# A five-engine kernel whose loop over passes is written out in full

## Chip, cores and metric

The kernel runs on one core of a Trainium2 chip. The metric is the time of one execution on the device, in microseconds. Five engines work side by side: TensorE (PE in the profile, PEld for its weight loads), VectorE (DVE), ScalarE (ACT), GpSimd (POOL) and SyncE (SP), which here issues all DMAs. Each has its own instruction stream, and they hand work to each other through semaphores.

## What is computed

Two transformer layers over 32 sequences of 256 rows with 128 features, each sequence on its own. Every sub-layer is followed by a residual sum and a layer norm:

```python
x = L0_attn_x                                   # (32, 256, 128)
x = _layernorm(x + _L0_attn_ref(x, ...))        # 16 heads of 8, softmax with a distance bias
x = _layernorm(x + _L0_ffn_ref(x, ...))         # 8 experts, top 2, and a shared one; silu(x W1) * (x W3) W2
x = _layernorm(x + _L1_attn_ref(x, ...))        # each row attends to rows at fixed distances; a sigmoid gate
x = _layernorm(x + _L1_ffn_ref(x, ...))         # 8 experts, top 2, one matrix each
return x
```

## The kernel before

One sequence's work is cut into stages, and the stages are laid over each other like a pipeline. `LAG` says how many passes after its start a sequence reaches a stage: `A1` (q, k, v and the scores for the row maximum) and `M` in pass e, `A2` and `A3` (first attention) in e + 1, `B` (experts of the first layer) in e + 2, `B2` in e + 3, `C1` and `C2` (second attention) in e + 3 and e + 4, `D` and `D2` (experts of the second layer) in e + 5 and e + 6. So one pass works on up to seven sequences, and 32 sequences take 38 passes. A pass runs `one(t, par, key)` on every engine: `t` is the pass, `par` its parity (some buffers are double), and `stages(t)` gives the sequence of each stage or None.

Within a pass each engine follows a fixed list of steps, `ORDER`. TensorE begins with `A1.qk` (L423, L424), `A1.v`, `B2.z` (L542) and `D2.y`; VectorE begins with `B2.res` (L956), then the steps of `A1` (L900 to L915), `D2.res` (L950) and `N.root` (L817 to L834), which computes the inverse roots of all four layer norms of the pass. From `n_r` and `n_b` that it gives, ACT normalises (L754), and TensorE transposes the result (L441) for the next stage.

Nothing synchronises the passes but these steps. Each engine counts its finished steps of a stage in a semaphore (`Steps`), and a waiting step waits for `count(e, step)`, which is `e` times the number of steps in a pass, plus the step's place. A finished DMA adds 16 (`dma_count`).

The passes stand in three parts. Passes 0 to 6 (`LOOP_FROM` is 7) are written out. Passes 7 to 30 are a loop on each engine, `eng.Fori`, of 12 turns with two passes each, since parity must be a constant. Passes 31 to 37 (`LOOP_TO` is 31) are written out again. In the loop `t` is an expression of the loop's register:

```python
with eng.Fori(0, (LOOP_TO - LOOP_FROM) // 2) as r:
    for u in range(2):
        one(r * 2 + (LOOP_FROM + u), (LOOP_FROM + u) % 2, LOOP_FROM + u)
```

so each wait's value, and the addresses of three DMAs on SP (`bass.ds(e * T, T)` and the like), are computed in registers while the kernel runs. `take` keeps for each PSUM bank who used it last, and in what pass; where the loop begins and ends its record is set to the loop's terms.

Of the kernel before, what the change touches and what calls it, by code (L numbers as in the profile page):

```python
# [6 lines left out]
B, T, D = 32, 256, 128  # L7
H, HD = 16, 8
E = 8
TT = T // 128  # L10
# [26 lines left out]

NORMS = ("A3n", "B2", "C2n", "D2")
LAST = max(LAG.values())
LOOP_FROM = LAST + 1  # L40
LOOP_TO = LOOP_FROM + (B - 1 - LOOP_FROM) // 2 * 2
Z_FIRST = 6
PV_ORDER = (0, 1, 4, 5, 2, 3, 6, 7)

# [51 lines left out]
def dma_count(e, per_run=1):  # L96

    return 0 if isinstance(e, int) and e < 0 else (e + 1) * (16 * per_run)


def network(nc, A, out):
# [4 lines left out]
    with ctx:  # L106
        def sb(name, shape, dt=F):
            return ctx.enter_context(nc.sbuf_tensor(name, shape, dt))
# [4 lines left out]
        def sem(name):  # L113
            return ctx.enter_context(nc.semaphore(name))
# [22 lines left out]
        xT = sb("xT", [128, T])  # L137
        x0, x2b = sb("x0", [128, TT, D]), sb("x2b", [128, TT, D])
# [13 lines left out]
        xout = sb("xout", [128, TT, D])  # L152
# [91 lines left out]
        ld_xT, ld_x = sem("ld_xT"), sem("ld_x")  # L244
        st_part, ld_stack, ld_m = [sem(f"st_part{n}") for n in range(3)], sem("ld_stack"), sem("ld_m")
        st_cB, ld_cB, st_cD, ld_cD = sem("st_cB"), sem("ld_cB"), sem("st_cD"), sem("ld_cD")
        st_w, ld_w, st_out = sem("st_w"), sem("ld_w"), sem("st_out")
# [11 lines left out]
        x_rows = A["x"].rearrange("b (t p) c -> p (b t) c", p=128)  # L259
        out_rows = out.rearrange("b (t p) c -> p (b t) c", p=128)  # L260
# [13 lines left out]
        def stages(t):  # L274

            r = {}
            for s, lag in LAG.items():
                e = t - lag
                r[s] = None if isinstance(e, int) and not 0 <= e < B + (LAG["D"] - lag if s == "G" else 0) else e
            return r  # L280
# [2 lines left out]

            return slice(0 if r["B"] is not None else 1, 2 if r["D"] is not None else 1)

        def passes(eng, one):


            for t in range(LOOP_FROM):
                one(t, t % 2, t)  # L290
            with eng.Fori(0, (LOOP_TO - LOOP_FROM) // 2) as r:
                for u in range(2):
                    one(r * 2 + (LOOP_FROM + u), (LOOP_FROM + u) % 2, LOOP_FROM + u)
            for t in range(LOOP_TO, B + LAST):
                one(t, t % 2, t)

        block = ctx.enter_context(nc.Block())
# [3 lines left out]
        def _(sp):  # L301
# [15 lines left out]
            def one(t, par, key):  # L317
                r = stages(t)
                for what, n in ORDER["sp"]:
# [2 lines left out]
                            sp.dma_start(dst[:], A[name]).then_inc(ld_expert, 16)  # L322
                    if what == "X.xT" and (e := r["X"]) is not None:
                        sp.wait_ge(peA1.sem, peA1.count(e - 1, "v"))
                        sp.dma_start(xT[:], A["xT"][:, bass.ds(e * T, T)]).then_inc(ld_xT, 16)
                    if what == "A3.x":
                        if (e := r["A3"]) is not None:
                            sp.wait_ge(dveA3.sem, dveA3.count(e - 1, "res"))
                            sp.dma_start(x0[:], x_rows[:, bass.ds(e * TT, TT), :]).then_inc(ld_x, 16)
                    if what == "A1.part" and (e := r["A1"]) is not None:  # L330

                        if n == 0:
# [51 lines left out]
                        sp.dma_start(stack[par][ROW_M:ROW_M + 1, 0], mT[:]).then_inc(ld_m, 16)  # L384
                    if what == "D2.out" and (e := r["D2"]) is not None:
                        sp.wait_ge(actND.sem, actND.count(e, "nm", 1))
                        sp.dma_start(out_rows[:, bass.ds(e * TT, TT), :], xout[:]).then_inc(st_out, 16)

            passes(sp, one)
            sp.wait_ge(st_out, dma_count(B - 1))  # L390


        @block.tensor
        def _(pe):
# [5 lines left out]
            last = {b: None for b in (0, 1, 2, 6, 7)}  # L400
# [6 lines left out]
                last[bank_no] = (*now, t)  # L407

            def one(t, par, key):
                if key == LOOP_FROM and not isinstance(t, int):  # L410
                    for b in last:
                        last[b] = (*last[b][:4], t - 1)
                if isinstance(t, int) and t == LOOP_TO:
                    for b in last:
                        last[b] = (*last[b][:4], LOOP_TO - 1)
                r = stages(t)
                odd = 1 - par
                for what, n in ORDER["pe"]:
# [205 lines left out]
                    if what == "M.mT" and (e := r["M"]) is not None:  # L624
# [5 lines left out]
                            i = nc.tensor.transpose(o[0:H, tt * 128:tt * 128 + 128], mneg[:, tt, :], identb[:])  # L630
                        i.then_inc(peM.done("mT"), 1)

            passes(pe, one)


        @block.scalar
        def _(act):
# [17 lines left out]
            def one(t, par, key):  # L655
# [3 lines left out]
                for what, n in ORDER["act"]:  # L659
# [103 lines left out]
                    if what == "M.mT" and (e := r["M"]) is not None:  # L763
                        act.wait_ge(peM.sem, peM.count(e, "mT"))
                        act.wait_ge(ld_m, dma_count(e - 1))
                        nc.scalar.copy(mT[:], b7[:].bitcast(BF)[0:H, 0:T]).then_inc(actM.done("mT"), 1)

            passes(act, one)


        @block.vector
        def _(dve):
# [273 lines left out]
                        dve.wait_ge(peM.sem, peM.count(e - 1, "mT"))  # L1046
                        v.tensor_scalar(mneg[:], mx[:], -1.0, None, ALU.mult).then_inc(dveM.done("neg"), 1)

            passes(dve, one)


        @block.gpsimd
        def _(pool):
# [50 lines left out]
                        tt_(h9[:, n, :].rearrange("p (t n) -> p t n", t=TT), ub[n % 2][:].rearrange("p (t n) -> p t n", t=TT),  # L1104
                            gB["cb"][:, :, expert(n), :], ALU.mult).then_inc(poolB.done("h", n - 1), 1)

            passes(pool, one)


def distance_tables():  # L1110
# [114 lines left out]
```

## Time and profile before

| | |
|---|---|
| Time of three runs | 1998.36, 2018.55 and 2006.53 us; median 2006.53 us |
| The profiled execution | 2014.43 us, of which 2012.6 us is the span of the program's own instructions |
| TensorE | busy 1601.7 us (80% of the span), mean granted clock 0.905 |
| VectorE | busy 1334.9 us (66%) |
| ACT | busy 922.6 us (46%) |
| POOL | busy 917.0 us (46%) |
| DMA | 214.15 MB, 106 GB/s; two of the queues, q8 and q14, carry instructions |

The time is that of one execution; the profile is another view of one such execution, on the only core used. In its rows a time in square brackets is how long the engine had been idle before, followed by what ended it; "issue" stands there where the profile shows nothing that was waited for. The granted clock (PEclk) is TensorE's share of its full 2.4 GHz; it takes two levels, 1.00 and 0.50, and in a stretch it is their mean.

### The profile page before, as it was taken

The page shows a single profiled execution, that of the slowest core. Times are in us where ns is not written, and L with a number is a line of the kernel's source. Part 1 is how long each engine was busy: PE and PEld are TensorE (multiplying, and loading weights), DVE is VectorE, ACT ScalarE, POOL GpSimd, SP SyncE. Part 2 cuts the span into 40 slices and gives each one's busy share as a digit, 9 for nine tenths or more (in the row PEclk, how much of TensorE's full clock was granted, in tenths as well). Part 3 has the DMA queues.
Part 4 walks back from the last instruction along what each step waited for, and adds up shares of the span by engine and source line. Part 5 has one row for each costly group of instructions (what it writes and reads, how often), then busy time and mean ns, then how long its engine had stood idle before and what let it go on. Part 6 is the DMA issues. An engine that isn't in the chain of part 4 may idle for free.

```text
span 2012.6 us, 41817 instructions
## 1 busy us (share of the span) xinstructions
PE 1601.7 (80%) x12928; PEld 1209.2 (60%) x12928; DVE 1334.9 (66%) x3466; ACT 922.6 (46%) x1868; POOL 917.0 (46%) x772
## 2 busy tenths in 40 slices
PE   1788888887888888888878878888888888886633
PEld 1466666665666666566666656666666666664523
DVE  2456777776757767576767767677677767775543
ACT  1355444454545445454535545554455545543310
POOL 0014355455535554553555455355545554455542
PEclk9899989898989989899989898999899989998755
DMA  5334444354544434454443444444344445433321
GB/s 102 86 90 106 95 113 109 98 125 107 129 107 117 115 91 115 102 128 107 118 113 94 112 107 129 109 120 118 87 112 123 115 118 128 106 95 92 92 71 50
DMA packets 86025, 214.15 MB, mean 106 GB/s; under 512 B 11634, under 2 KB 68210, under 8 KB 68594
## 3 DMA queue, kind: packets, MB, share of 16 engines
q1 hardware_dynamic: 85844, 211.96, 42.6%
q8 instruction: 87, 1.43, 0.4%
q14 instruction: 94, 0.77, 0.2%
HBM read 185.97 MB, written 25.69 MB: 105 GB/s over the span
## 4 chain that ended last, share of the span: by engine, by line
PE 33%; issue 20%; POOL 15%; DMA 13%; DVE 10%; ACT 5%; SPq 3%; DVEq 0%; POOLq 0%; ACTq 0%
POOL prod L1079 7%; DMA d_parts<-parts 6%; DMA stack<-d_parts 5%; PE b L521 4%; PE bPV L542 3%; POOL h L1104 3%; DVE mx L1005 3%; PE bS L559 3%; PE bTU L571 3%; POOL prod L1095 3%; PE bTU L572 2%; PE b L580 2%; PE bTU L491 2%; POOL wb L1070 2%; PE bPV L510 2%
## 5 line engine op out<-in xcount | busy, mean ns | idle before, releaser
L1005 DVE TENSOR_REDUCE mx<-bS 128x2 f32<-128x512 f32 x512 | 337.0, 684 | 204.9 <-PE bS L562 202.4
L1079 POOL TENSOR_TENSOR prod<-kC,qC 128x512 f32<-128x512 f32 x256 | 363.7, 1451 | 142.2 <-ACT kC L683 142.2
L1104 POOL TENSOR_TENSOR h<-ub,gBcb 128x256 f32<-128x256 f32 x256 | 185.1, 729 | 422.3 <-DVE ub L1018 370.3
L1070 POOL TENSOR_TENSOR wb<-wb 128x1024 f32<-128x1024 f32 x64 | 162.6, 2541 | 417.3 <-DVE wb L923 417.3
L714 ACT ACTIVATE P<-bTU 128x512 f32<-128x512 f32 x512 | 276.8, 606 | 27.6 <-PE bTU L494 22.4
L559 PE MATMUL bS<-stack 96*128 96x256 bf16 x1024 | 232.8, 296 | 65.9 <-DMA stack<-d_parts 21.5
L723 ACT ACTIVATE sil<-bTU,b 128x256 f32<-128x256 f32 x288 | 136.7, 474 | 299.5 <-PE bTU L572 134.2
L571 PE MATMUL bTU<-x1T,w 128*128 128x256 f32 x576 | 203.5, 437 | 50.5 <-DVE h L1018 49.9
L491 PE MATMUL bTU<-stack 97*128 97x256 bf16 x1024 | 237.8, 284 | 4.9 <-ACT P L714 3.8
L494 PE MATMUL bTU<-dist,identh 128*128 128x128 f16 x1024 | 213.0, 226 | 0.0
L562 PE MATMUL bS<-dist,identh 128*128 128x128 f16 x1024 | 210.2, 233 | 0.0
L923 DVE TENSOR_TENSOR wb<-wb,vC 128x512 f32<-128x512 f32 x256 | 174.0, 731 | 45.1 <-DMA wb<-d_w 44.7
L559 PEld LDWEIGHTS bS<-stack 96*128 96x128 bf16 x1024 | 106.7, 104 | 154.2 <-DVE mx L1005 68.6
L572 PE MATMUL bTU<-x1T,w 128*128 128x256 f32 x576 | 185.3, 405 | 0.0
L1095 POOL TENSOR_TENSOR prod<-gDcb,x3T 128x512 f32<-128x512 f32 x128 | 160.6, 1267 | 34.1 <-DMA gDcb<-d_cD 34.1
L542 PE MATMUL bPV<-w,h 128*128 128x128 f32 x1152 | 154.0, 287 | 19.8 <-POOL h L1104 19.8
L521 PE MATMUL b<-ew,prod 128*128 128x128 f32 x1024 | 147.6, 299 | 17.1 <-POOL prod L1095 17.1
L542 PEld LDWEIGHTS bPV<-w,h 128*128 128x128 f32 x1152 | 143.7, 201 | 25.0 <-POOL h L1104 24.8
L521 PEld LDWEIGHTS b<-ew,prod 128*128 128x128 f32 x1024 | 135.5, 211 | 24.7 <-POOL prod L1095 14.3
L510 PE MATMUL bPV<-P,Vz 128*32 128x256 f32 x2048 | 148.0, 410 | 0.7 <-ACT P L714 0.7
L571 PEld LDWEIGHTS bTU<-x1T,w 128*128 128x128 f32 x576 | 94.1, 204 | 67.1 <-DVE h L1018 57.2
L491 PEld LDWEIGHTS bTU<-stack 97*128 97x128 bf16 x1024 | 106.1, 104 | 40.6 <-ACT P L714 26.4
(159 smaller groups left out, 2909.2 us busy)
## 6 DMA issues: line engine op xcount, KB each, us to landing
wb<-d_w SPq DMA_DIRECT2D x32, 2048.0 KB, 12.5
gBcb<-d_cB SPq DMA_DIRECT2D x32, 1024.0 KB, 4.8
gDcb<-d_cD SPq DMA_DIRECT2D x32, 1024.0 KB, 4.7
stack<-d_parts SPq DMA_DIRECT2D x288, 64.0 KB
stack<-d_parts SPq DMA_DIRECT2D x96, 192.0 KB
d_parts<-parts SPq DMA_DIRECT2D x96, 128.0 KB, 7.7
d_w<-wT SPq DMA_DIRECT2D x32, 256.0 KB
xT<-in_xT SPq DMA_DIRECT2D x32, 128.0 KB, 4.6
```

What stands on the lines that cost most here:

```text
L491: mm(o[:, q], stack[odd][0:ROW_M + 1, 1, h, kt * 128:kt * 128 + 128], stack[odd][0:ROW_M + 1, 0, h, :], start=True, stop=False)
L494: i = mm(o[:, c], identh[:], dist[:, h, 0, :], start=False, stop=last_part)
L521: i = mm(b6[:, tt * 128:tt * 128 + 128], xs[:, x, tt * 128:tt * 128 + 128], ew[:, x, :], start=(x == 0), stop=(x == E - 1))
L542: i = mm(bPV[:, tt * 128:tt * 128 + 128], h9[:, x, tt * 128:tt * 128 + 128], w2[:, expert(x), :], start=False, stop=(x == E), skip_group_c ...
L559: mm(o[:, qt * T:qt * T + T], stack[par][0:ROW_M, 0, h, qt * 128:qt * 128 + 128], stack[par][0:ROW_M, 1, h, :], start=True, stop=False)
L571: mm(bAB[:, 0:T], w13[:, x, 0, :], x1T[:], start=True, stop=True)
L572: mm(bAB[:, T:2 * T], w13[:, x, 1, :], x1T[:], start=True, stop=True).then_inc(peB.done("ab", n), 1)
L714: act_f(P[k % 8][:].rearrange("p a b -> p (a b)"), bTU[turn_bank("ST", k)][:], ACT.Exp).then_inc(actA2.done("exp", k), 1)
L1005: v.tensor_reduce(mx[:, :, k], bS[k % 2][:].rearrange("p (a b) -> p a b", a=TT), op=ALU.max, axis=AX.X).then_inc(dveA1.done("max", k), 1)
L1079: tt_(prod[:, 2 * p:2 * p + 2, :], shifted(kC, p), qC[:].unsqueeze(1).to_broadcast([128, 2, T]), ALU.mult).then_inc(poolC1.done("prod", p), 1)
L1095: tt_(xs[:, 2 * i:2 * i + 2, :].rearrange("p x (t n) -> p x t n", t=TT), gD["cb"][:, :, 2 * i:2 * i + 2, :].rearrange("p t x n -> p x t n" ...
L1104: tt_(h9[:, n, :].rearrange("p (t n) -> p t n", t=TT), ub[n % 2][:].rearrange("p (t n) -> p t n", t=TT), gB["cb"][:, :, expert(n), :], ALU ...
```

## The change

The loop is gone. `passes` calls `one(t, t % 2, t)` for t from 0 to 37 in Python, so all 38 passes are written out on each engine; `t` and `e` are plain numbers. There is no branch, no register arithmetic, every wait is on a constant and every DMA has a constant address. The corrections of `last` at the loop's ends are dropped, since the record of the banks is right by itself. The steps, their order, buffers, tiles and DMAs are the same.

```diff
-        def passes(eng, one):
-
-
-            for t in range(LOOP_FROM):
-                one(t, t % 2, t)
-            with eng.Fori(0, (LOOP_TO - LOOP_FROM) // 2) as r:
-                for u in range(2):
-                    one(r * 2 + (LOOP_FROM + u), (LOOP_FROM + u) % 2, LOOP_FROM + u)
-            for t in range(LOOP_TO, B + LAST):
+        def passes(one):
+
+            for t in range(B + LAST):
                 one(t, t % 2, t)
...
-                        sp.dma_start(xT[:], A["xT"][:, bass.ds(e * T, T)]).then_inc(ld_xT, 16)
+                        sp.dma_start(xT[:], A["xT"][:, e * T:e * T + T]).then_inc(ld_xT, 16)
...
-                            sp.dma_start(x0[:], x_rows[:, bass.ds(e * TT, TT), :]).then_inc(ld_x, 16)
+                            sp.dma_start(x0[:], x_rows[:, e * TT:e * TT + TT, :]).then_inc(ld_x, 16)
...
-                        sp.dma_start(out_rows[:, bass.ds(e * TT, TT), :], xout[:]).then_inc(st_out, 16)
+                        sp.dma_start(out_rows[:, e * TT:e * TT + TT, :], xout[:]).then_inc(st_out, 16)
...
-                if key == LOOP_FROM and not isinstance(t, int):
-                    for b in last:
-                        last[b] = (*last[b][:4], t - 1)
-                if isinstance(t, int) and t == LOOP_TO:
-                    for b in last:
-                        last[b] = (*last[b][:4], LOOP_TO - 1)
...
-            passes(pe, one)
+            passes(one)
```

Two places show what becomes of the instruction streams. In these rows a `REGISTER_ALU` or `ISA` row is register arithmetic, some of it with a wait in it, and square brackets name the semaphores waited for.

TensorE at the end of the loop's body, before: the last matmuls of a turn (`B.ab.8`) and the branch back.

```order
L630 MATMUL b<-identb,mneg 16x128 [waits dveM,actC1]
L630 MATMUL b<-identb,mneg 16x128
L406 REGISTER_ALU
L571 MATMUL bTU<-x1T,w 128x256 [waits dveB]
L572 MATMUL bTU<-x1T,w 128x256
L291 REGISTER_ALU
L291 COMPARE_AND_BRANCH
```

TensorE at the start of the loop's body, before, where the branch leads: `A1.qk`, `A1.v` and the first of `B2.z`.

```order
L291 ISA
L422 ISA [waits dveA3]
L423 MATMUL b<-xT,wqk 128x256 [waits ld_xT]
L424 MATMUL b<-xT,wqk 128x256
L406 REGISTER_ALU
L429 MATMUL b<-wv,xT 128x128 [waits actM]
L429 MATMUL b<-wv,xT 128x128
```

TensorE at the same boundary of two passes, after: lines are numbered 14 less.

```order
L557 MATMUL bTU<-x1T,w 128x256 [waits dveB]
L558 MATMUL bTU<-x1T,w 128x256
L409 MATMUL b<-xT,wqk 128x256 [waits ld_xT,dveA3]
L410 MATMUL b<-xT,wqk 128x256
L415 MATMUL b<-wv,xT 128x128 [waits actM]
L415 MATMUL b<-wv,xT 128x128
L528 MATMUL bPV<-w,h 128x128 [waits poolB]
```

The branch and the register instructions are gone, and the matmuls of one pass follow on those of the pass before in one stream.

VectorE ahead of `N.root` in the loop, before: the end of the moments of `D2.res`, then four register instructions with the waits for the norms' inputs, then the first steps of the inverse root.

```order
L810 BN_AGGR n_mv<-nDst 128x2
L962 ISA
L962 REGISTER_ALU [waits actNA,dveA3]
L962 ISA [waits actNB,dveBn]
L964 ISA [waits dveC2n]
L817 TENSOR_SCALAR n_v<-n_mv 128x8 [waits actND,dveDn,actNC]
L818 ISA
L819 TENSOR_SCALAR n_i<-n_v 128x8 [waits dveN]
L820 REGISTER_ALU
L821 TENSOR_SCALAR n_r<-n_i 128x8 [waits dveN]
```

VectorE at the same place, after.

```order
L796 BN_AGGR n_mv<-nDst 128x2
L803 TENSOR_SCALAR n_v<-n_mv 128x8 [waits dveC2n,actNC,actNB,dveDn,dveBn,actND,actNA,dveA3]
L805 TENSOR_SCALAR n_i<-n_v 128x8 [waits dveN]
L807 TENSOR_SCALAR n_r<-n_i 128x8 [waits dveN]
L813 TENSOR_TENSOR n_s<-n_r 128x8 [waits dveN]
```

All eight semaphores are now waited for on constants, directly ahead of the first instruction of `N.root`.

## Rows read from the trace of the kernel before

**Rows 1.** The page: busy time of the engines, and the chain that ended last.

```profile
PE 1601.7 (80%) x12928; PEld 1209.2 (60%) x12928; DVE 1334.9 (66%) x3466; ACT 922.6 (46%) x1868; POOL 917.0 (46%) x772
...
PE 33%; issue 20%; POOL 15%; DMA 13%; DVE 10%; ACT 5%; SPq 3%; DVEq 0%; POOLq 0%; ACTq 0%
```

**Rows 2.** Busy time by stretches: passes 6, 7, 10, 18, 19, 25, 28, 31; 7 to 30.

```profile
core 0: us, PE busy (x) PEld busy (x) DVE busy (x) ACT busy (x) POOL busy (x), PEclk, DMA share, GB/s
...
291.30:346.90 55.60, 47.24 (x407) 36.06 (x406) 41.67 (x105) 27.70 (x58) 28.93 (x25) 0.97 0.50 118
346.90:405.80 58.90, 51.38 (x406) 38.77 (x406) 40.49 (x106) 28.61 (x58) 28.64 (x25) 0.88 0.46 110
...
520.40:579.50 59.10, 48.10 (x407) 36.50 (x407) 40.55 (x106) 28.72 (x58) 31.22 (x27) 0.94 0.54 131
...
988.20:1052.60 64.40, 51.13 (x406) 39.03 (x405) 42.79 (x105) 28.72 (x58) 31.15 (x27) 0.90 0.51 122
...
1052.60:1106.10 53.50, 45.81 (x406) 35.01 (x406) 40.78 (x105) 28.67 (x58) 26.10 (x22) 1.00 0.38 99
...
1395.40:1456.80 61.40, 52.54 (x405) 39.04 (x405) 40.38 (x106) 28.66 (x58) 28.63 (x25) 0.86 0.43 105
...
1568.30:1621.80 53.50, 46.05 (x407) 34.88 (x406) 41.13 (x105) 28.73 (x58) 28.96 (x25) 1.00 0.48 120
...
1737.40:1790.90 53.50, 44.94 (x398) 33.83 (x397) 40.17 (x106) 27.11 (x54) 29.04 (x25) 0.99 0.49 119
...
346.90:1737.40 1390.50, 1178.27 (x9698) 893.54 (x9698) 984.01 (x2521) 689.71 (x1393) 690.09 (x577) 0.93 0.45 113
```

**Rows 3.** Waits of TensorE and VectorE, 343 to 1734 us: us, times, longest us.

```profile
PE b L423 <- issue: 26.6, 6, 5.0
...
DVE n_v L817 <- issue: 14.7, 5, 4.1
```

**Rows 4.** Timeline of TensorE, 454 to 462 us: start us, us.

```profile
455.69 0.59 PE L572 MATMUL bTU<-x1T,w 128*128 128x256 f32 x2
460.28 1.22 PE L423 MATMUL b<-xT,wqk 128*128 128x256 f32 x2 [4.00 <-issue]
```

**Rows 5.** Timeline of TensorE, 689.5 to 692 us.

```profile
690.13 0.59 PE L572 MATMUL bTU<-x1T,w 128*128 128x256 f32 x2
690.57 0.59 PE L423 MATMUL b<-xT,wqk 128*128 128x256 f32 x2
```

**Rows 6.** DMA queues, 690:920, 924:1160, 60:343 us: packets, MB, share.

```profile
q1 hardware_dynamic: 10134, 25.73, 45.4%
q14 instruction: 12, 0.10, 0.2%
...
q8 instruction: 18, 0.29, 0.6%
...
q8 instruction: 16, 0.26, 0.4%
```

**Rows 7.** Timelines of VectorE in passes 13, 19 and 31.

```profile
703.08 0.17 DVE L817 TENSOR_SCALAR n_v<-n_mv 128x8 f32<-128x8 f32 x1 [2.60 <-issue]
...
705.50 0.17 DVE L834 SCALAR_TENSOR_TENSOR n_b<-n_mv,n_r 128x8 f32<-128x8 f32 x1
...
1058.87 0.17 DVE L817 TENSOR_SCALAR n_v<-n_mv 128x8 f32<-128x8 f32 x1 [0.82 <-DVE n_mv L810]
...
1743.39 0.17 DVE L817 TENSOR_SCALAR n_v<-n_mv 128x8 f32<-128x8 f32 x1 [0.23 <-DVE n_mv L810]
...
1745.81 0.17 DVE L834 SCALAR_TENSOR_TENSOR n_b<-n_mv,n_r 128x8 f32<-128x8 f32 x1
```

**Rows 8.** Timelines of TensorE in passes 13, 28 and 31: the first L441.

```profile
707.49 0.44 PE L441 MATMUL b<-ident,x 128*128 128x128 f32 x2 [3.08 <-ACT x L754]
...
1578.89 0.41 PE L441 MATMUL b<-ident,x 128*128 128x128 f32 x2 [0.77 <-ACT x L754]
...
1747.80 0.41 PE L441 MATMUL b<-ident,x 128*128 128x128 f32 x2 [0.61 <-ACT x L754]
```

More of the change, by code:

```diff
@@ L39 @@
 LAST = max(LAG.values())
-LOOP_FROM = LAST + 1
-LOOP_TO = LOOP_FROM + (B - 1 - LOOP_FROM) // 2 * 2
 Z_FIRST = 6
@@ L386, in one @@
                         sp.wait_ge(actND.sem, actND.count(e, "nm", 1))
-                        sp.dma_start(out_rows[:, bass.ds(e * TT, TT), :], xout[:]).then_inc(st_out, 16)
-            passes(sp, one)
+                        sp.dma_start(out_rows[:, e * TT:e * TT + TT, :], xout[:]).then_inc(st_out, 16)
+            passes(one)
             sp.wait_ge(st_out, dma_count(B - 1))
@@ L631, in one @@
                         i.then_inc(peM.done("mT"), 1)
-            passes(pe, one)
+            passes(one)
         @block.scalar
@@ L766, in one @@
                         nc.scalar.copy(mT[:], b7[:].bitcast(BF)[0:H, 0:T]).then_inc(actM.done("mT"), 1)
-            passes(act, one)
+            passes(one)
         @block.vector
@@ L1047, in one @@
                         v.tensor_scalar(mneg[:], mx[:], -1.0, None, ALU.mult).then_inc(dveM.done("neg"), 1)
-            passes(dve, one)
+            passes(one)
         @block.gpsimd
@@ L1105, in one @@
                             gB["cb"][:, :, expert(n), :], ALU.mult).then_inc(poolB.done("h", n - 1), 1)
-            passes(pool, one)
+            passes(one)
 def distance_tables():
```

## Prediction, made before the changed kernel was run

> **What bounds the kernel now.** I read the page first, then the busy time by stretches, then the waits of TensorE and VectorE, then the timelines around one turn of the loop. TensorE is busy 80% of the span, yet the chain that ended last is only 33% TensorE and 20% "issue", time in which an engine waits for nothing that the profile shows [rows 1]. So no engine is full. The time is the length of a pass, and that is set by engines handing work to each other. I cut the trace into passes at VectorE's `B2.res` (L956), the first thing VectorE does in a pass: the stretch from one L956 to the next I call by its pass number t. Passes 7 to 30 are the loop, two to a turn; 0 to 6 and 31 to 37 are already written out in the kernel before. That is what makes a prediction possible: passes 6 and 31 do the full work with no loop (31 lacks only the load of the next x).
>
> The 24 passes of the loop take 1390.5 us [rows 2], 57.94 us each. They are far from equal, 53.4 to 64.4 us. Pass 6 takes 55.6 us and pass 31 takes 53.5 us [rows 2]. What tells long from short is seen in two places.
>
> First place, TensorE at the loop's turn. Six times in the loop its first matmul of a turn (`A1.qk`, L423) waits for "issue", 26.6 us in all; one of these is the first pass of a turn after 455.69 us, where TensorE stands still for 4.00 us [rows 3, 4]. There are 11 backward jumps. At the other five the first matmul follows without a gap [rows 5]. The explanation that fits is code fetch: in 924 to 1160 us, with two stalled turns, the core moves 18 packets on the instruction queue q8, and in 690 to 920 us, with turns that do not stall, q8 does not appear at all [rows 6]. q8 is then TensorE's code, and the loop's body at times stays on the engine and at times has to be fetched again. The stall has an after-effect. The two half-matmuls of L423 take 1.22 us together after it and 0.59 us after a turn without it [rows 4, 5], so the granted clock fell to 1.2 GHz from 2.4 after the idle time. The six passes that end in such a stall (8, 10, 16, 18, 20, 22) take 59.1 (pass 10) to 64.4 us (pass 18), 62.1 us on average [rows 2].
>
> Second place, VectorE after a turn at which TensorE did not stall. Five times its `N.root` (L817) waits for "issue", 14.7 us in all [rows 3]: in pass 13 it starts at 703.08 us, after 2.60 us of idleness [rows 7]. In pass 19 the same instruction waited 0.82 us and in pass 31, without a loop, 0.23 us [rows 7]. VectorE, too, lacks code; when TensorE has stalled longer, VectorE's fetch is over before its inputs come, so it shows only in the other turns. What hangs on it: ACT's normalising step L754, and behind that TensorE's transpose L441, which idles 3.08 us here against 0.61 us in pass 31 [rows 8]. These five passes (13, 15, 25, 27, 29) take 57.1 to 61.4 us, 59.9 us on average; pass 25 is the longest, at a granted clock of 0.86 [rows 2].
>
> The other 13 passes of the loop take what is left: 1390.5 - 6 x 62.1 - 5 x 59.9 = 718.4 us, 55.3 us each. Six of them follow a TensorE stall and are flattered, since POOL, ACT and the queue had time to get ahead (54.6 us on average; pass 19 is one, 53.5 us [rows 2]). The seven that had no such help average 55.9 us.
>
> **The change part by part.** **The jumps.** 11 backward jumps and one that falls through go. Six passes come down from 62.1 to the 55.9 us of a pass that is neither hurt nor helped: 6 x 6.2 = 37 us. Five come down from 59.9: 5 x 4.0 = 20 us. The six helped passes lose their help: 6 x 1.3 = -8 us. Net of the jumps: 49 us.
>
> The Trainium skill prices a jump differently. "Advanced Engine Details and Errata", section Control Flow Timing, gives about 108 ns for a compare-and-branch; an estimate by that figure alone is 12 x 0.11 = 1.3 us for the whole kernel, that is no change. The rows above with their 4.00 us decide against it as the whole price of a jump.
>
> **The register arithmetic.** A turn of the loop has 152 register instructions on TensorE, 140 on ACT, 197 on VectorE, 42 on POOL and 41 on SP, most of them one `REGISTER_ALU` or `ISA` ahead of a wait. Most cost nothing: the sequencer does them while the instruction before runs. From L817 to L834, thirteen short instructions with a register instruction ahead of nearly each, it takes 2.42 us in the loop (703.08 to 705.50) and 2.42 us written out (1743.39 to 1745.81) [rows 7]. The cover is the 0.17 us of the instruction itself. Where several stand in a row they do show: L817 has four ahead of it and idles 0.82 us in odd passes of the loop against 0.23 us [rows 7], and TensorE's L441 behind it idles 0.77 us in pass 28 against 0.61 us in pass 31 [rows 8]. The bounds for this edit are zero and about 1 us a pass (0.6 at L817 plus a few tenths at the two later handovers). I take 0.6 us a pass, near the L817 row, since that wait is on the path of every pass: 24 x 0.6 = 14 us.
>
> **The added instructions.** A wait on a register's value was partly folded into the register instruction; written out, an instruction carries one wait on a constant and each further wait is an instruction of its own. Passes 6 and 31 contain these already and are no longer than the loop's passes without a stall, so I add nothing. Nothing is moved from one place to another, and DMAs are the same in number, order and size.
>
> **The longer code.** Written out, every engine fetches all its code once. For TensorE that is about 4 packets of 16 KB a pass: 16 packets in 60 to 343 us, where five to six passes run [rows 6], so about 95 for the 24 passes. In those 283 us no TensorE or VectorE wait for "issue" stands in the view of the waits, and none in 1734 to 2012 us. Bounds: nothing, by these stretches; 4.0 us plus a fall of the clock for each fetch that comes late, by rows 4. I take nothing.
>
> "Runtime: NRT & Kernel Launch", section Instruction fetch mechanics, in the Trainium skill, says that straight code is fetched ahead block by block and mostly hidden, and that only a jump outside the window makes an engine wait. By it the last term is nothing too, but it would have TensorE stall at all 11 jumps, and the trace shows six.
>
> **The sum.** The profiled execution took 2014.43 us for a span of 2012.6 us. 2014.4 - 49 - 14 = 1951 us. Put otherwise, 24 passes of 55.3 us in place of 57.94. The profiled execution lies 0.4% above the median of the three runs (2006.53 us), so the median to expect is 1951 x 2006.53 / 2014.43 = 1943 us.
>
> **The rivals.** **(A) The passes cannot get shorter on average.** A stall of one pass is partly given back in the next: a stalled pass and its successor take 116.6 us together, a turn without TensorE stall 115.3 us. If other waits fill the holes, as in passes 6 and 7, which have no jump before them and take 55.6 + 58.9 = 114.5 us, the gain is 12 x (115.9 - 114.5) = 17 us, and the median 1990 us. For it: passes 5, 7 and 11 are 58 to 59 us long without any stall, pass 7 at a granted clock of 0.88 [rows 2]. Against it: passes 30 and 31 take 108.9 us together. In this rival I put also that a jump costs only itself.
>
> **(B) The even flow.** Pass lengths settle at the floor that passes 19, 28 and 31 show, 53.5 us [rows 2], with the clock near full throughout. Then 2014.4 - 24 x 4.44 = 1908 us, and the median 1900 us. It needs that no wait of TensorE lets the clock fall; pass 6, with the shorter waits of written-out code, still ran at 0.97.
>
> **(C) Slower: straight code is fetched too late.** TensorE waits for the next 16 KB where it has run quickly through a block of short matmuls. The price of one is that of the stall at a jump, 6.2 us with its fall of the clock, on 95 fetches. The gain of 63 us is eaten when 10 of them are late, and the kernel is over 1% slower from 14 on. With 16 late ones the median is 1943 + 99 = 2042 us. Against it stands that none of the 16 fetches in the first written-out stretch was late [rows 6].
>
> **How the numbers follow.** Forecast (passes of 54.4 to 56.6 us on average, 1922 to 1974 us) 0.60; B and what lies between it and the forecast 0.15; A and what lies between 0.22; C 0.03. The likeliest is the forecast, 1943 us. The range reaches to most of B and A: passes of 53.7 and 57.05 us give 1905 and 1985 us. One per cent of 2006.5 is 20 us, about what a measurement of this kernel can tell from no change (the three runs span 20 us). Faster by over 1% means under 1986 us: the forecast, B and half of A, 0.86. Within 1%: the rest of A, 0.11. Slower: 0.03.
>
> **What would show it right or wrong.** In the changed kernel's profile: no wait for "issue" before the first `A1.qk` matmul of a pass nor before `N.root`; instruction packets on q8 evenly through the span, some 100 or more; passes between 53.5 and 58 us with no 60s; a mean granted clock over the middle above the 0.93 of the loop; TensorE's transpose L441 (now L427) idle 0.6 us or so in each pass. The prediction is wrong if the passes with clock falls that have no stall today (7, 11) turn out to be the rule, for which the granted clock would stay at 0.93 or below, or if new "issue" waits stand in the middle of passes.

## The result, and the profile after

The written-out kernel takes 1943.86 us (median of 4 runs, 1937.71 to 1946.21) against 2011.99 us for the kernel before (4 runs). The ratio is 0.9665, 95% interval 0.9604 to 0.9727. The forecast was 1943 us. All ratios here and below leave out a few slow executions (the furthest out are 2913 and 4914 us of the kernel before beside e1 to e4, and 2045 us of e3).

The profiled execution took 1946.21 us. The page: the span, busy time, the granted clock in tenths by 40 slices, the two instruction queues and the chain that ended last.

```profile
span 1944.4 us, 36324 instructions
...
PE 1559.3 (80%) x12928; PEld 1180.2 (61%) x12928; DVE 1346.3 (69%) x3466; ACT 922.0 (47%) x1868; POOL 921.7 (47%) x772
...
PEclk9799889999999999999999999999999999997755
...
q8 instruction: 103, 1.69, 0.4%
q14 instruction: 77, 0.63, 0.1%
...
PE 34%; DMA 30%; DVE 18%; issue 7%; SPq 5%; ACT 4%; POOL 3%; POOLq 0%; DVEq 0%; ACTq 0%
```

Beside [rows 1], "issue" on the chain falls from 20% to 7% and DMA rises from 13% to 30%. That alone doesn't show that the path has moved off the instruction streams. The chain is one path picked from a closely coupled kernel, and it can jump: e4 below has no wait of TensorE or VectorE for "issue" in its middle and still has 26% of it.

```profile
POOL 28%; issue 26%; PE 22%; DVE 9%; DMA 7%; ACT 6%; SPq 1%; POOLq 1%; ACTq 0%; DVEq 0%
```

What follows rests on pass lengths and waits.

Busy time by stretches after: passes 7 to 30, then the longest (18) and the shortest of them (24).

```profile
core 0: us, PE busy (x) PEld busy (x) DVE busy (x) ACT busy (x) POOL busy (x), PEclk, DMA share, GB/s
345.80:1667.60 1321.80, 1133.82 (x9699) 863.25 (x9698) 991.59 (x2521) 687.89 (x1393) 693.96 (x577) 0.97 0.48 118
949.70:1008.00 58.30, 47.35 (x407) 35.98 (x406) 42.49 (x106) 28.73 (x59) 28.71 (x25) 0.97 0.46 110
1285.50:1337.60 52.10, 45.74 (x406) 34.77 (x405) 40.80 (x106) 28.67 (x59) 28.88 (x25) 1.00 0.50 126
```

The middle went from 1390.5 [rows 2] to 1321.8 us, 68.7 us less: 55.07 us a pass. The rest of the program hardly moved: up to pass 7, 346.9 before and 345.8 after; pass 31, 53.5 and 56.0; what follows, 221.7 and 220.8. Of the 68.7 us, TensorE's busy time gave 1178.3 - 1133.8 = 44.5 us with the same matmuls, and its idle time 24.2 us. So nearly two thirds of the gain stands in TensorE's busy time, in matmuls that run at a higher granted clock, 0.97 in place of 0.93.

Waits of TensorE and then of VectorE after, 343 to 1668 us: us, times, longest us.

```profile
PE bS L545 <- DMA stack<-d_parts: 37.1, 21, 3.5
PE bTU L557 <- DVE h L1004: 34.9, 24, 1.6
PE b L427 <- ACT x L740: 14.7, 24, 0.6
...
DVE nBy L942 <- PE bPV L528: 61.6, 25, 2.5
DVE wb L909 <- DMA wb<-d_w: 42.0, 24, 3.0
```

The waits for "issue" of [rows 3] are gone from both engines (what is left in the middle, weight loads aside, is 1.1 us in three waits of VectorE at L831, and 0.2 us once on VectorE and once on ACT), and the transpose waits 0.6 us in every pass. At the top stands a wait that was small before: `bS`, the scores for the row maximum, waits for the rows of q and k that went out to memory (`d_parts`) and come back (`stack`). In passes 7 to 30 of the kernel before it was 7.5 us in 7 waits; now it is 37.1 in 21.

```profile
PE bS L559 <- DMA stack<-d_parts: 7.5, 7, 2.2
```

Passes 18 and 24 differ by 6.2 us, and about half of that is this wait: in 18 it takes 3.2 us, and in 24 it does not occur.

Timelines of VectorE and TensorE in pass 24: start us, us.

```profile
1291.53 0.17 DVE L803 TENSOR_SCALAR n_v<-n_mv 128x8 f32<-128x8 f32 x1 [0.23 <-DVE n_mv L796]
...
1295.94 0.41 PE L427 MATMUL b<-ident,x 128*128 128x128 f32 x2 [0.60 <-ACT x L740]
```

These are the 0.23 and the 0.6 us of pass 31 in [rows 7, 8], now in the middle of the run.

### The profile page after: what moved, and what is told of

It is laid out like the page before. It is cut to its first block, busy times and chain, and to the rows that moved or that the text cites. A ratio compares the mean times of both kernels' runs of the same rounds, so it can differ in the third digit from the quotient of the medians.

```text
span 1944.4 us, 36324 instructions
## 1 busy us (share of the span) xinstructions
PE 1559.3 (80%) x12928; PEld 1180.2 (61%) x12928; DVE 1346.3 (69%) x3466; ACT 922.0 (47%) x1868; POOL 921.7 (47%) x772
## 4 chain that ended last, share of the span: by engine, by line
PE 34%; DMA 30%; DVE 18%; issue 7%; SPq 5%; ACT 4%; POOL 3%; POOLq 0%; DVEq 0%; ACTq 0%
DMA d_parts<-parts 14%; DMA stack<-d_parts 13%; DVE mx L991 6%; PE bPV L528 5%; PE bS L545 4%; PE bTU L557 4%; PE bTU L558 4%; PE b L566 3%; SPq L337 3%; DVE wb L955 2%; DVE wb L960 2%; PE bS L548 2%; DMA wb<-d_w 2%; PE b L507 2%; POOL prod L1065 1%
## 5 line engine op out<-in xcount | busy, mean ns | idle before, releaser
L545 PE MATMUL bS<-stack 96*128 96x256 bf16 x1024 | 236.9, 300 | 90.1 <-DMA stack<-d_parts 50.1
L709 ACT ACTIVATE sil<-bTU,b 128x256 f32<-128x256 f32 x288 | 136.5, 474 | 335.9 <-PE bTU L558 180.1
L557 PE MATMUL bTU<-x1T,w 128*128 128x256 f32 x576 | 206.5, 443 | 47.5 <-DVE h L1004 47.1
L477 PE MATMUL bTU<-stack 97*128 97x256 bf16 x1024 | 229.9, 278 | 3.6 <-ACT P L700 2.7
L909 DVE TENSOR_TENSOR wb<-wb,vC 128x512 f32<-128x512 f32 x256 | 173.0, 727 | 66.7 <-DMA wb<-d_w 61.5
L480 PE MATMUL bTU<-dist,identh 128*128 128x128 f16 x1024 | 208.4, 222 | 0.0
L558 PE MATMUL bTU<-x1T,w 128*128 128x256 f32 x576 | 187.5, 410 | 0.0
L528 PE MATMUL bPV<-w,h 128*128 128x128 f32 x1152 | 148.3, 279 | 19.7 <-POOL h L1090 19.7
L528 PEld LDWEIGHTS bPV<-w,h 128*128 128x128 f32 x1152 | 136.9, 192 | 26.0 <-POOL h L1090 25.8
L496 PE MATMUL bPV<-P,Vz 128*32 128x256 f32 x2048 | 140.0, 392 | 0.7 <-ACT P L700 0.7
L1004 DVE SCALAR_TENSOR_TENSOR ub<-bTU,b,sil 128x256 f32<-128x256 f32 x256 | 118.2, 472 | 19.4 <-ACT sil L709 18.5
## 6 DMA issues: line engine op xcount, KB each, us to landing
wb<-d_w SPq DMA_DIRECT2D x32, 2048.0 KB, 12.4
```

The costliest lines, as they stand in the source:

```text
L477: mm(o[:, q], stack[odd][0:ROW_M + 1, 1, h, kt * 128:kt * 128 + 128], stack[odd][0:ROW_M + 1, 0, h, :], start=True, stop=False)
L480: i = mm(o[:, c], identh[:], dist[:, h, 0, :], start=False, stop=last_part)
L528: i = mm(bPV[:, tt * 128:tt * 128 + 128], h9[:, x, tt * 128:tt * 128 + 128], w2[:, expert(x), :], start=False, stop=(x == E), skip_group_c ...
L545: mm(o[:, qt * T:qt * T + T], stack[par][0:ROW_M, 0, h, qt * 128:qt * 128 + 128], stack[par][0:ROW_M, 1, h, :], start=True, stop=False)
L557: mm(bAB[:, 0:T], w13[:, x, 0, :], x1T[:], start=True, stop=True)
L558: mm(bAB[:, T:2 * T], w13[:, x, 1, :], x1T[:], start=True, stop=True).then_inc(peB.done("ab", n), 1)
```

## The experiments

All start from the kernel before, but for e8 and e9, which start from the changed one. `passes` is given the engine's name, and an engine that isn't in the list is written out as in the change. Every kernel does the whole computation. Two figures stand for each: the time with the ratio to the kernel before of the same chip, and the length of passes 7 to 30 in the profile (1390.5 before, 1321.8 after). The kernel before took 2014.9 us beside e1 to e4, 2014.3 beside e5 to e8 and 2008.9 beside e9 to e11. Where I compare two experiments with each other, I take the difference of their ratios as a share of 2012 us, and the root of the summed squares of their intervals. The middle is read from one execution, and that one need not be typical: in e1 and e2 the profiled execution was the fastest of all (1957.87 of five, 1990.81 of ten), so their middles are on the low side.

**e1 to e3: a loop on one engine, or on the three quiet ones.**

```diff
-        def passes(eng, one):
+        def passes(eng, one, name):
+            looped = name in ("pe",)          # e2: ("dve",)   e3: ("act", "pool", "sp")
+            for t in range(LOOP_FROM if looped else B + LAST):
+                one(t, t % 2, t)
+            if looped:
+                with eng.Fori(0, (LOOP_TO - LOOP_FROM) // 2) as r:
...
```

e1, TensorE alone loops. 

> Only TensorE runs passes 7 to 30 as a loop of 12 turns; the other four engines are written out. Theory (code fetch at the jump): TensorE stalls about 4.4 us at 6 to 11 of the 11 backward jumps, each worth 6.2 us with the fall of the clock, less what the next pass gains: 1943.9 us (the written-out kernel) plus 30 to 55, so 1974 to 1999 us, with an issue wait before A1.qk in the profile. Rival (register arithmetic is the cost): TensorE's share of it is hidden under matmuls, so no more than 5 us above, 1949 us at most.

Measured: 1969.31 us, 0.9787 (0.9753 to 0.9822); middle 1333.9 us. Waits of TensorE:

```profile
PE b L424 <- issue: 24.3, 6, 4.5
```

It came out 5 us below the range of my theory and 20 us above the rival's. The six stalls are there as before, though the other engines have no loop: they are TensorE's own. Against the written-out kernel the loop costs 25 us, give or take 14. In the profiled execution it costs only 12 us in the middle, half of its 24.3 us of stall: the six stalled passes take 59.9 us on average, but each next one 52.5 us, 2.6 us less than a written-out pass. So a part of each stall is made up at once.

e2, VectorE alone loops. 

> Only VectorE runs passes 7 to 30 as a loop. Theory: N.root waits for code in nearly all 11 turns now that TensorE never stalls, 4.0 us of pass time each (44 us), and VectorE's register arithmetic ahead of N.root costs up to 0.6 us a pass (14 us): about 1995 us. Rival (register arithmetic alone): 14 us above 1943.9, 1958 us, and no issue wait at N.root.

Measured: 2008.05 us, 0.9977 (0.9943 to 1.001); middle 1365.2 us, clock 0.94. Waits of VectorE:

```profile
DVE n_v L818 <- issue: 38.5, 11, 4.4
```

More than either theory gave: VectorE's loop alone costs 63 us, give or take 14, nearly the whole gain (43 us in the middle of the profiled execution). `N.root` now stalls at all 11 turns, against five in [rows 3]. The instruction queue q14 shows what happened at the other six. The page of the kernel before, of e2 and of e3 below:

```profile
q14 instruction: 94, 0.77, 0.2%
```

```profile
q14 instruction: 121, 0.99, 0.2%
```

```profile
q14 instruction: 50, 0.41, 0.1%
```

Written out, q14 carries 77 packets. A loop on VectorE adds 121 - 77 = 44 packets where the other engines are written out, and 94 - 50 = 44 where they loop too. So in the kernel before VectorE fetched its code as often as here, also at the turns where no stall of `N.root` shows. As the prediction has it, TensorE's stall at a turn gave VectorE's fetch time to end; where TensorE doesn't stop, VectorE's stall is bare.

e3, ACT, POOL and SP loop. 

> Only ACT, POOL and SP loop (bodies of 290, 95 and 96 instructions), with their register arithmetic. Theory: these bodies stay on their engines, so no stall at a jump, and the register instructions are mostly hidden: 1944 to 1950 us. Rival (register arithmetic ahead of every wait costs a few tenths at each handover, ACT's and SP's above all): 1960 us or more.

Measured: 1957.59 us, 0.9722 (0.9675 to 0.9768); middle 1328.1 us, no wait for "issue" above 0.4 us in it. Between both theories: 14 us over the 1943.9, where I had expected next to none. By the ratios it is 11 us, give or take 16, and 6 us in the middle of the profile, so a cost is likely but not separated from none.

The three costs are 25, 63 and 11 us by the ratios, 99 together, and all five loops cost 67. The excess of 31 us is uncertain by 28, and the profiled middles, 12, 43 and 6 us, sum to 62, less than the 69 of all five. That the costs of the loops are smaller together is therefore not settled by the times. That VectorE's stall hides behind TensorE's is seen in the waits and in q14.

**e4, e7, e11: the loop stays, the jump is announced.** The loop takes a hint that its backward jump will be taken; the program is the same otherwise. e4 has it on all five engines, e7 loops VectorE alone, e11 TensorE alone.

```diff
-                with eng.Fori(0, (LOOP_TO - LOOP_FROM) // 2) as r:
+                with nc.Fori(0, 12, engines=type(mybir.ALL_ENGINES)([eng.engine]), hint_back_edge=True) as r:
```

e4: 

> The kernel before with its loop on all five engines and all register arithmetic, but each engine announces the backward jump at the top of a turn (a branch prefetch hint), so that the target's code is fetched before it is needed. Theory: the stalls at the jumps go and the register arithmetic stays: 1943.9 plus 14, about 1958 us. Rival one (the register arithmetic is most of the cost): 1990 us or more. Rival two (the hint's fetch pushes other code of the body off the engine, so that stalls only move): about 2005 us, with issue waits elsewhere.

Measured: 1980.58 us, 0.9852 (0.9808 to 0.9896). Busy time by stretches: passes 7 to 30, and pass 31.

```profile
345.60:1691.00 1345.40, 1164.93 (x9697) 882.88 (x9696) 978.51 (x2520) 688.30 (x1393) 693.13 (x577) 0.94 0.47 115
1691.00:1756.70 65.70, 53.23 (x398) 39.28 (x398) 39.95 (x105) 27.31 (x55) 28.82 (x25) 0.84 0.43 104
```

Slower than expected, for two reasons. The hint is wrong once, where the loop is left: pass 31 takes 65.7 us against 56.0. Two engines stall for "issue" in it, both some way behind the loop's end: ACT 16 us after its last branch, in the normalising step that TensorE's transpose waits for (3.6 us there, 0.6 written out), and VectorE 56 us after its own.

```profile
1703.87 0.49 ACT L757 ACTIVATE x<-nAy,n_b,n_r 128x128 f32<-128x128 f32 x1 [2.91 <-issue]
...
1743.64 0.88 DVE L1021 SCALAR_TENSOR_TENSOR ub<-bTU,b,sil 128x256 f32<-128x256 f32 x2 [3.40 <-issue]
```

And inside the loop, where TensorE and VectorE now have no wait for "issue", the passes are still 23.6 us longer than written out. This kernel splits the change in two. From before to e4 the middle loses 1390.5 - 1345.4 = 45.1 us: that is the stalls at the jumps. From e4 to after it loses 23.6 us: that is the register instructions and whatever an announced jump still costs. The times agree: by the ratios, with pass 31 set aside, the two steps are 42 and 28 us.

Of the 23.6 us TensorE's busy time is 1164.9 - 1133.8 = 31.1 us, and its idle time goes the other way by 7.5 us: e4 has less of it (180.5 us against 188.0) and yet a granted clock of 0.94, not 0.97. So the sum of idle time doesn't tell the clock here. Nor is the loss spread over all passes. The 12 odd passes, each the first of a turn, take 56.97 us on average at a clock of 0.92; the 12 even ones take 55.15 us at 0.96. Written out it is 55.13 and 55.02 us. Some 22 of the 23.6 us lie in the odd passes, and there `N.root` idles 0.83 us and the transpose waits 1.3 us; in the even ones it is 0.40 and 0.77 us, with next to no loss. An odd pass has the longer register chain ahead of `N.root`, and it also stands behind the announced jump. No run parts these two.

e7: 

> Only VectorE loops, with its backward jump announced at the top of each turn. Beside the loop on VectorE without the hint (2008 us) it tells the price of VectorE's missing code from that of its register arithmetic. Theory: the waits at N.root go, VectorE's register arithmetic stays (up to 14 us) and the last turn, where the announced jump is not taken, may stall once: 1955 to 1968 us. Rival (VectorE's loss is its register arithmetic): near 2000 us with no issue wait at N.root.

Measured: 1964.06 us, 0.9781 (0.9707 to 0.9855); middle 1334.9 us, pass 31 61.9 us. Waits of VectorE:

```profile
DVE n_v L820 <- issue: 16.3, 10, 2.2
```

The time is as expected, the waits are not: they were to go, and 10 are left. Against e2 the hint takes the stall from 38.5 to 16.3 us and the kernel from 2008 to 1964 (39 us by the ratios, give or take 16). VectorE still fetches: q14 carries 111 packets here, 34 above the written-out 77, and 84 in e4, 34 above the 50 of e3. So the fetches were there in e4 too, but no stall at `N.root` shows; why is open. Pass 31 is 6 us longer than written out, with a stall of 3.7 us at the same place as VectorE's in e4.

e11: 

> Only TensorE loops, with its backward jump announced. Beside the loop on TensorE without the hint (25 us above the written-out kernel) it tells TensorE's six stalls from its register arithmetic. Theory: no stall before A1.qk, register arithmetic hidden under matmuls, one stall where the loop ends as in the other runs with hints: 1946 to 1958 us. Rival (register arithmetic): near 1969 us again, without issue waits.

Measured: 1936.5 us, 0.9645 (0.9612 to 0.9679); middle 1315.4 us, no wait of TensorE for "issue". Better than expected and level with the written-out kernel (0.9665, 0.9604 to 0.9727); the stall that I expected where the loop ends did not come, and pass 31 takes 55.1 us. So TensorE's register arithmetic costs nothing that can be measured, and what e1 loses is its six stalls: e1 and e11 differ by the hint alone, and by 29 us, give or take 10. The page says how the hint works on this engine, e1 first, e11 second, and e10 below, with seven stalls, third:

```profile
q8 instruction: 87, 1.43, 0.3%
```

```profile
q8 instruction: 33, 0.54, 0.1%
```

```profile
q8 instruction: 96, 1.57, 0.4%
```

In e11 passes 0 to 6 and 31 to 37 take 26 of the 33 packets, and the middle 7, one fetch of the loop's body. Each stall then adds nine packets, and a turn without a stall none: 33 + 6 x 9 = 87 in e1 and in the kernel before, 33 + 7 x 9 = 96 in e10. So the body stays on the engine at every turn of e11, and without the hint it is fetched anew at just those turns where TensorE stalls.

**e5: six loops of two turns.** Six jumps backward in place of 11, the register instructions as before.

```diff
+                for k in range(6):
+                    at = LOOP_FROM + k * 4
+                    with nc.Fori(0, 2, engines=type(mybir.ALL_ENGINES)([eng.engine]), hint_back_edge=False) as r:
+                        for u in range(2):
+                            one(r * 2 + (at + u), (LOOP_FROM + u) % 2, LOOP_FROM + u)
```

> Passes 7 to 30 on all engines as six loops of two turns each (two passes a turn) in place of one loop of 12 turns: 6 backward jumps in place of 11, the register arithmetic of all 24 passes kept. Theory (a jump costs some 4 us of the span, the register arithmetic about 24 us in all, from the run with hints): 1944 + 24 + 6 x 4.1, about 1992 us, a ratio of 0.989 to the kernel before. Rival (what costs is the register arithmetic or the loop form, not the jumps): 2010 us or more, a ratio of 0.998 to 1.002.

Measured: 1991.77 us, 0.9907 (0.9869 to 0.9946); middle 1367.4 us. Waits of TensorE, then of VectorE:

```profile
PE b L426 <- issue: 15.2, 3, 5.6
```

```profile
DVE n_v L820 <- issue: 3.3, 1, 3.3
DVE n_s L830 <- issue: 2.0, 1, 2.0
```

A hit: 22.5 us gained for five jumps less, 4.5 us a jump; by the ratio 19 us, give or take 8, so 2 to 5 us a jump. The rival's 2010 us lies outside. The waits of both engines for "issue" fall with it, from 41.3 us [rows 3] to 20.5 in the rows above.

**e6: ACT alone loops**, to find where e3's cost lies (the list is `("act",)`). 

> Only ACT loops; its body of 290 instructions gave no stall in the run where ACT, POOL and SP looped, which was 11 us above the written-out kernel. Theory (ACT has 70 register instructions a pass and stands in most handovers to TensorE): most of the 11 us is ACT's, 1950 to 1956 us. Rival (it is POOL's and SP's): within 2 us of 1944 us.

Measured: 1953.6 us, 0.9703 (0.9643 to 0.9763); middle 1331.6 us. The time lies in the range of my theory, but the intervals of e6, e3 and the written-out kernel overlap, so it stays open how much of e3's cost is ACT's. What shows is small: the transpose, which waits for ACT's normalising step, waits 0.71 us in odd passes and 0.62 in even ones, against 0.61.

**e8, e9, e10: the new wait.** After the change the longest wait of TensorE is for `stack<-d_parts`. SP's timeline shows what stands before it in the queue:

```profile
1060.14 0.55 SPq L372 DMA_DIRECT2D wb<-d_w  x1
1061.57 0.37 SPq L329 DMA_DIRECT2D d_parts<-parts  x1
...
1065.62 1.15 SPq L329 DMA_DIRECT2D d_parts<-parts  x2
1072.79 2.31 SPq L337 DMA_DIRECT2D stack<-d_parts  x7
```

`wb<-d_w` brings 2048 KB for the second attention and lands 12.4 us after its issue. The three small writes behind it, 128 KB each, take 8.4 us (page, DMA issues; the median of all three). e8 starts from the changed kernel and cuts that load in two: slots 0 to 3 and 8 to 11 where it stood, the others in a new SP step `C2.wb` behind the three writes; VectorE waits for the second half at its fifth product.

```diff
-        A1.part.0 A3.x A1.part.1 A1.part.2 A1.rows.0 ...
+        A1.part.0 A3.x A1.part.1 A1.part.2 C2.wb A1.rows.0 ...
...
+        def wb_half(sp, half, s):
+            for at in (4 * half, 4 * half + 8):
+                sp.dma_start(wb[:, at:at + 4, :].rearrange("p s n -> p (s n)"),
+                             bass.AP(d_w.tensor, at * T, [[NS * T, H], [0, HD], [1, 4 * T]])).then_inc(s, 16)
...
+                        if n == 4:
+                            dve.wait_ge(ld_w2, dma_count(e, 2))
```

> The written-out kernel with its largest load cut in two: the first half of wb (4 of the 8 products of C2.pv) is issued where the whole was, the second half after the three writes of parts to d_parts. In the written-out kernel the 2 MB of wb take 12.4 us and the writes issued behind them land after 11 us, and TensorE's scores then wait for stack. Theory (the written-out kernel is bound by this DMA queue): the rows of stack come 3 us earlier and the wait of VectorE for wb goes, 1 to 1.5 us a pass on 32 passes: 1900 to 1915 us. Rival (the same bytes must pass before the scores anyway, or the clock or VectorE takes over): 1935 to 1944 us. It could be slower, if the second half comes late for VectorE's fifth product: up to 1960 us.

Measured: **1892.27 us**, 0.9421 (0.936 to 0.9482); middle 1285.5 us, 53.56 us a pass. The page's DMA issues of the changed kernel and of e8 (KB each, us to landing):

```profile
wb<-d_w SPq DMA_DIRECT2D x32, 2048.0 KB, 12.4
...
d_parts<-parts SPq DMA_DIRECT2D x96, 128.0 KB, 8.4
```

```profile
wb<-d_w SPq DMA_DIRECT2D x128, 512.0 KB, 6.1
...
d_parts<-parts SPq DMA_DIRECT2D x96, 128.0 KB, 3.2
```

Better than expected. The writes land in 3.2 us, and over the whole run the wait for `stack` falls from 50.1 to 27.1 us, while VectorE's wait for `wb` does not grow (61.5 to 54.8). The best kernel of this study. The edit does two things: it puts half of the load behind the writes, and it makes four loads of 512 KB of one of 2 MB. No run has the four loads in the old place, so the share of each is open.

e9 moves the whole load behind the writes instead of half of it. 

> The written-out kernel with all of wb (2 MB in one load) issued after the three writes of parts instead of ahead of them. It tells whether the order in the DMA queue alone made the gain of the split. Theory (the writes of parts stood behind wb in one queue): the writes land in about 5 us in place of 11, but wb now lands some 5 us later and VectorE waits longer for it before C2.pv, so a part of the split's gain of 52 us is lost: 1905 to 1935 us. Rival (the split gains by the smaller transfers, not by the order): 1944 us or more.

Measured: 2162.69 us, 1.0771 (1.0736 to 1.0806); middle 1518.8 us. Waits of VectorE over the whole run, and the page's DMA issues:

```profile
DVE wb L908 <- DMA wb<-d_w: 281.2, 32, 11.3
```

```profile
wb<-d_w SPq DMA_DIRECT2D x32, 2048.0 KB, 13.5
...
d_parts<-parts SPq DMA_DIRECT2D x96, 128.0 KB, 1.9
```

A miss of over 200 us. Order alone does bring the writes in first, after 1.9 us, but the first slots of `wb` stand on VectorE's path: it waits 8.8 us for them in each of 32 passes, and others wait behind it (ACT 229.3 us for VectorE's `gdl`, and TensorE 179.2 us for ACT's `kC`). By e8, the second half had time to spare.

e10 puts e8's split into the kernel before, with its loops. 

> The kernel before, loop and register arithmetic and all, with wb split as in the fastest run. Theory (the waits for code and the wait for the DMA queue cover each other in part, since the chain of the kernel before is 13% DMA and that of the written-out one 30%): the split gains less here than the 52 us it gained written out: 1975 to 1995 us. Rival (the two gains add): 2012 - 52, about 1960 us.

Measured: 1967.96 us, 0.979 (0.9752 to 0.9828); middle 1364.4 us. Waits of TensorE:

```profile
PE b L431 <- issue: 30.0, 7, 4.9
```

I had expected the split to be worth less in the loop. The time, 1967.96 us, lies 7 us below my range and 8 us above the rival's 1960. The split is worth 42 us here, give or take 8, and 49 us written out, give or take 17, so by the times the gains may add. The profiles part them: 18 to 20 us of the gain lie outside the loop, in passes that are written out in both kernels (346.9 to 335.9 us up to pass 7 here, 345.8 to 336.1 in e8, and 8 to 9 us from pass 31 on in each). In the middle the split saves 26 us with the loop and 36 without it. So it is worth less there, as expected, though by less than I thought. And it saves those 26 us while the wait for `stack` stays as it was (7.5 and 8.3 us): a wait's own size doesn't bound what lies behind it. Through which handover it is saved was not followed up.

## Why the prediction was right, step by step

**The number.** 1943 forecast, 1943.9 measured. That the two meet within 1 us is luck: the forecast was scaled to a median of 2006.5 us for the kernel before, which came to 2012.0 with the fourth run, and the gain was 68 us where 63 were forecast. In its own terms: 24 passes of 55.3 us were forecast, and 55.07 came, from 52.1 to 58.3 (53.5 to 58 was the sign given) with no 60s. Rival A (1990), B (1900) and C (2042) all lie outside the measured runs.

**The jumps, 49 us.** The stalls at the jumps gave 45.1 us (before against e4), or 4.1 us for each of 11. TensorE's part, six stalls less the help that they give to the pass behind, was 37 - 8 = 29 us in the prediction; put back alone it costs 25 us (e1), and the hint takes 29 us of it away (e1 against e11). Both steps of that reading show in e1: long passes at the stalls, and short ones behind them. VectorE's part was 20 us for five turns. It can't be measured in the presence of TensorE's stalls, but its mechanism was tested: the prediction says that VectorE fetches at the other turns too and is covered there, and e2 has the stall at all 11 turns, with the same 44 extra packets on q14 as in the kernel before. Bare, it is the dearer of the two: VectorE's loop costs 63 us with its register instructions, and the hint, which leaves 16.3 of the 38.5 us of stall, takes 39 us of that away (e2 against e7, give or take 16).

**The register arithmetic, 14 us.** This is the term that was mis-sized: it was 23.6 us by e4 against the change, with what remains of an announced jump in it; the bound given was 24 (1 us a pass). The reading under it is also wrong. The prediction names the odd passes as those with 0.82 us at L817 and then takes 0.6 us for all 24; in even passes L817 idles 0.40 us, so against 0.23 us the loop costs 0.6 us in every second pass and 0.2 in the others, 9 us in 24 passes. For the transpose the prediction took an even pass (0.77 us), and an odd one without a stall has 1.3 us against 0.61. "0.6 us on the path of every pass" is neither. That 14 came nearer to 23.6 than 9 would have is chance. What was left out is what e4 shows in the odd passes: a delay of 0.6 to 0.7 us comes with a pass that is 1.8 us longer and a clock of 0.92 in place of 0.96. By engines only this is shown: TensorE's cost nothing (e11); for ACT, POOL and SP together 11 us, give or take 16 (e3).

**The added wait instructions, 0.** None shows. Written out, the same short chain of VectorE has the gaps it had in pass 31.

**The longer code, 0.** q8 carried 103 packets, "some 100" as forecast, and no matmul and no instruction of another engine waits more than 0.5 us for "issue" in the middle. The 95 packets given for the 24 passes do not follow from the prediction's own row, which gives about 3 a pass; 77 came, and 26 outside. Rival C asked for late fetches and there were none. The Trainium skill's page "Runtime: NRT & Kernel Launch", section Instruction fetch mechanics, calls a block boundary in straight code mostly hidden; the trace agrees, with 103 packets on q8 and no stall. Its rule that a jump outside the window forces a fetch and a stall fits VectorE in e2 (11 of 11 turns); on TensorE only 6 of 11 turns stall and fetch in e1, so at the others the target was still at hand.

**Rival A, filled holes.** Its mechanism is real, though it did not decide: the wait for `stack<-d_parts` grew from 7.5 to 37.1 us in the middle, 1.2 us a pass, and the passes behind a stall in e1 are shorter than written-out ones. Rival B's floor of 53.5 us a pass was not reached by this change; e8, which cuts that wait, runs at 53.56 us a pass. That the wait is what kept this kernel above the floor is likely and not shown, since e8 gains more than the wait was.

**The sum of the errors.** The jumps were put 4 us too high and the registers 10 us too low, which leaves 68.7 us in the middle against 63 forecast. Pass 31 became 2.5 us longer (53.5 to 56.0), which the forecast had at nothing. The two terms were right together more than apart.

**What is open.** Why TensorE's body stays on the engine at five turns and not at the other six. e11 shows that it can stay at all of them. Whether the 23.6 us are register instructions alone, since the passes that lose are the ones behind the jump; a run with the long register chain in the even pass would tell. And which part of e8's gain comes from the order of the loads and which from their size.

## What to carry to other kernels

Look at the first instructions after a backward jump for idle time that ends in "issue", on each engine by itself, since one engine's stall hides another's: here a jump cost about 4 us. Packets on the instruction queues show fetches that no wait shows. Where engines wait for each other closely, write the loop out, or announce the jump, which on TensorE alone gave as much at a third of its code traffic, but on all five engines (e4) gave less than half of the gain. After such a change read the waits anew: small writes queued behind a 2 MB load were worth another 50 us; moving the whole load behind them cost over 200. Don't take the shares of the chain for a measure of what a wait costs, and look at odd and even passes by themselves before you call one row typical.

## What the runs showed of the hardware

- **The hint keeps a loop's code on TensorE.** 33 packets of 16 KB on q8 in e11 against 87 in e1, nine for each of its six stalls. Where the loop is left, TensorE alone loses nothing (pass 31 takes 55.1 us in e11); in e4 ACT stalls 2.91 us and VectorE 3.40, and that pass is about 10 us longer.
- **VectorE fetches again at every turn.** 121 packets on q14 in e2 against 77 written out, and 94 against 50 where the other engines loop too; bare, the stall was 38.5 us in 11 turns. The hint leaves 34 of the 44 extra packets and 16.3 us of the stall (e7).
- **A DMA lands later for the bytes queued ahead of it.** The same write of 128 KB landed after 8.4 us behind a 2 MB load, 3.2 us behind half of it (2.3 in e10), 1.9 us ahead of it.
- **A lower granted clock costs busy time, and the sum of idle time doesn't foretell it.** The same matmuls of passes 7 to 30 took 1178.3 us at a mean granted clock of 0.93 (before), 1164.9 at 0.94 (e4) and 1133.8 at 0.97 (after), with 212.2, 180.5 and 188.0 us of idle time beside them.
